# Emptyings ahead of the sum, and more pairs between the steps of a tile, in an attention kernel with four chained stages

## What is computed

```python
h      = x @ W[cat] + b[cat]                       # cond, weights chosen per sequence
q,k,v  = split(h @ w_qkv.T)                        # 16 heads of 32
s      = q k^T / sqrt(32) - |i - j| * slope, masked to -10000 above the diagonal
num    = 0.5 * (1 + s * rsqrt(1 + s*s))            # in the place of exp
attn   = (num / (sum(num) + 1e-6)) @ v ; x1 = x + attn @ w_out.T
z      = layernorm(x1 + relu(x1 @ W1 + b1) @ W2 + b2) * gamma + beta
out    = x1 + int8_matmul(round(z / scale), weight_int8) * scales + bias
```

## Time and profile before

| | |
|---|---|
| median of 3 runs | 2193.9 us (2190.4 to 2200.6) |
| the profiled execution | 2191.51 us, of which the span of instructions is 2189.8 us |
| mean granted TensorE clock | 0.929 of 2.4 GHz |
| busy: PE, DVE, ACT, POOL | 1778.5, 1736.8, 1709.5, 1693.0 us |
| HBM | 31 GB/s over the span |

### The profile page before, as it was taken

How to read it: one execution, slowest core, us unless ns; L and a number is a source line. 1 busy time by engine, 2 the same in 40 slices (tenths; PEclk the granted TensorE clock), 3 DMA queues, 4 the chain that set the end, 5 groups by cost and what they waited for, 6 DMA issues and landing times.

```text
span 2189.8 us, 29394 instructions
## 1 busy us (share of the span) xinstructions
PE 1778.5 (81%) x10699; PEld 901.2 (41%) x10702; DVE 1736.8 (79%) x1730; ACT 1709.5 (78%) x1842; POOL 1693.0 (77%) x723
## 2 busy tenths in 40 slices
PE   5678888888887879997786887888888788988764
PEld 4455434333333445654343443433333344444231
DVE  4248888988999878977555777899999898879748
ACT  0037999999999978977554777999999998889652
POOL 3037899999989968877554776899998998889648
PEclk9899999999999989999988999999999999999889
DMA  5411111111111112212211212011111113112146
GB/s 182 150 50 41 46 31 31 42 38 35 36 35 45 31 56 64 60 41 61 68 44 47 81 50 64 24 44 40 36 32 36 41 31 90 42 57 58 59 160 204
DMA packets 122139, 130.38 MB, mean 60 GB/s; under 512 B 27372, under 2 KB 77548, under 8 KB 121580
## 3 DMA queue, kind: packets, MB, share of 16 engines
q1 hardware_dynamic: 121996, 128.51, 21.0%
HBM read 45.89 MB, written 22.54 MB: 31 GB/s over the span
## 4 chain that ended last, share of the span: by engine, by line
PE 34%; ACT 28%; DVE 17%; issue 11%; POOL 4%; SPq 3%; DMA 2%; DVEq 0%; POOLq 0%; ACTq 0%
ACT yb L765 11%; ACT gb L730 8%; ACT yb L767 8%; DVE gb L1094 6%; PE sc L943 6%; PE ov L921 6%; DVE gb L1159 5%; PE dn L921 5%; PE it L859 4%; PE it L866 4%; PE it L839 3%; SPq L479 3%; POOL oT L724 2%; PE it L843 2%; DMA area<-in_x_dram 1%
## 5 line engine op out<-in xcount | busy, mean ns | idle before, releaser
L691 POOL TENSOR_TENSOR yb<-yb 128x1024 f32<-128x1024 f32 x544 | 1503.6, 2776 | 384.8 <-DVE gb L1159 369.0
L1159 DVE TENSOR_TENSOR gb<-sc,yb 128x1024 f32<-128x1024 f32 x544 | 663.3, 1219 | 170.2 <-ACT yb L767 165.6
L765 ACT ACTIVATE yb<-sc 128x1024 f32<-128x1024 f32 x544 | 550.7, 1012 | 265.0 <-PE sc L943 157.9
L1094 DVE TENSOR_TENSOR gb<-gb,yb 128x1024 f32<-128x1024 f32 x544 | 753.8, 1386 | 0.0
L943 PE MATMUL sc<-qmv,kst 128*128 128x512 f32 (+3 forms) x1280 | 479.7, 458 | 175.0 <-DVE gb L1159 160.7
L767 ACT ACTIVATE yb<-yb 128x1024 f32<-128x1024 f32 x544 | 575.6, 1058 | 17.2
L730 ACT ACTIVATE gb<-gb 128x1024 f32<-128x1024 f32 x544 | 566.2, 1041 | 0.0
L943 PEld LDWEIGHTS sc<-qmv,kst 128*128 128x128 f32 x1280 | 230.6, 202 | 492.9 <-DVE gb L1159 342.8
L921 PE MATMUL ov<-gb,vv 128*32 128x512 f32 (+3 forms) x2560 | 320.0, 584 | 30.2 <-DVE den L1108 22.6
L921 PE MATMUL dn<-gb,ones 128*32 128x512 f32 (+3 forms) x2560 | 310.5, 568 | 0.0
L839 PE MATMUL it<-hT,wT 128*128 128x512 f32 x496 | 249.4, 608 | 14.4 <-ACT area L742 8.5
(11 more groups left out here) (118 smaller groups left out, 1087.9 us busy)
## 6 DMA issues: line engine op xcount, KB each, us to landing
qmv<-stage SPq DMA_DIRECT2D x384, 64.0 KB
kst<-stage SPq DMA_DIRECT2D x384, 64.0 KB
area<-in_x_dram SPq DMA_DIRECT2D x58, 256.0 KB, 2.8
out_dram<-oT SPq DMA_DIRECT2D x32, 256.0 KB, 3.2
wT<-wT_d SPq DMA_DIRECT2D x7, 768.0 KB, 4.3
x_d<-area SPq DMA_DIRECT2D x16, 256.0 KB, 2.6
z_d<-area SPq DMA_DIRECT2D x16, 256.0 KB, 2.9
gb<-z_d SPq DMA_DIRECT2D x4, 1024.0 KB, 12.2
```

The costliest lines, as they stand in the source:

```text
L691: pool.tensor_tensor(y, y, y, ALU.mult).then_inc(s_y2, 1)
L765: act.activation(yview(n), sc[:, n % SLOTS], ACT.Square).then_inc(s_s2, 1)
L1094: dve.tensor_tensor(gview(n), gview(n), yview(n), ALU.add).then_inc(s_num, 1)
L1159: dve.tensor_tensor(gview(n), sc[:, n % SLOTS], yview(n), ALU.mult).then_inc(s_g, 1)
```

## The change

EVAC goes from 1 to 2 and NORMED from 2 to 3: each step of a tile is placed at least two pairs behind the one it needs (zt three pairs behind norm), as far as due pairs allow. On ACT the emptyings of a pair now stand ahead of (1 + g) squared. On DVE the order becomes: product(k-1), outputs, emptyings of pair k, sum(k-3), inversions, product(k). Between the sums and products nothing is moved against each other; what moves are the emptyings and outputs, which now come ahead of the sum. The last three sums instead of two are left for the end.

```diff
-EVAC = 1
-NORMED = 2
+EVAC = 2
+NORMED = 3
...
                     act.activation(yview(n), yview(n), ACT.Abs_reciprocal_sqrt, bias=1.0).then_inc(s_y, 1)
-                    if n >= NUM_LAG:
-                        one_plus_g_squared(n - NUM_LAG)
                     for job in after_pair.get(k, []):
                         d = b if g is ending else b - 1
                         after(d, job, bases[0] + job.index, zs_before(d, job.name[1]))
+                    if n >= NUM_LAG:
+                        one_plus_g_squared(n - NUM_LAG)
...
-                def scored(k):
+                def product(k):
 
                     n = G * PAIRS + k
                     if n >= GRING:
                         dve.wait_ge(s_pv, products_until(n - GRING))
                     dve.wait_ge(s_y, n + 1)
                     dve.tensor_tensor(gview(n), sc[:, n % SLOTS], yview(n), ALU.mult).then_inc(s_g, 1)
+                    for u in emptied.pop(k, []):
+                        c = g.last_unit.index(u % UNITS)
+                        if u >= 0:
+                            output(G, hg, g, u, c, g is opening and c == 0)
+                        else:
+                            output_prev(G, prev_hg, u, c)
+
+                def rest(k):
+
+                    n = G * PAIRS + k - 1
                     if n >= NUM_LAG:
                         numerator(n - NUM_LAG)
                     while reduced and reduced[0][0] < k:
...
+                emptied = {}
                 k = None
                 for e in g.events:
-                    if e[0] in ("qk", "pv") and k is not None:
-                        scored(k)
-                        k = None
                     if e[0] == "qk":
+                        if k is not None:
+                            rest(k)
+                            product(k)
                         k = e[1]
...
                     elif e[0] == "pv":
                         u = e[1]
-                        if u < 0 and not carry:
-                            continue
-                        if u % UNITS in g.last_unit:
-                            c = g.last_unit.index(u % UNITS)
-                            if u >= 0:
-                                output(G, hg, g, u, c, g is opening and c == 0)
-                            else:
-                                output_prev(G, prev_hg, u, c)
-                if k is not None:
-                    scored(k)
+                        if (u >= 0 or carry) and u % UNITS in g.last_unit:
+                            emptied.setdefault(k, []).append(u)
+                rest(k)
+                product(k)
...
-            for n in range(TOTAL - NUM_LAG, TOTAL):
+            for n in range(TOTAL - NUM_LAG - 1, TOTAL):
                 numerator(n)
```

## The result

| | before | after |
|---|---|---|
| median of 4 runs each, same chip | 2192.9 us | 2311.8 us (2311.5 to 2312.8) |
| ratio, 95% interval | | 1.0537 (1.051 to 1.0563) |
| the profiled execution, and its span | 2191.5, 2189.8 us | 2312.8, 2311.0 us |
| mean granted TensorE clock | 0.929 | 0.913 |

What follows compares the result with a forecast made beforehand. ACT was taken to bound plain groups, PE was busiest in closing, joining waited in chains. Plain +15, opening +8, closing +3, joining +10.5, ending +7 gave +43: 2234.5 us, 2237 against the median; range 2184 to 2268.

Steps and rivals of the forecast that it cites:

- part 1: DVE's emptyings ahead of the sum, all groups: sums meet POOL's y squared; plain +15, opening +8, closing +3, joining +8, ending +4.
- part 3: Longer lags in joining and ending: waits for inputs go (-5, -8; -3), forced rows cost (+16, +8, +1.5; +12).
- Of a plain group's 16 emptyings I count 10, since the others fall beside an existing stall.: Plain groups: only 10 emptyings delay the next square, 10 x 0.6 = 6.0 us per group before the outputs' gain.
- 0.6 us late, whether the emptying is short or long: At a moved emptying the sum ends 1.95 us later against 1.34 of slack, so the next square starts 0.6 late.
- covers ACT's delay: Closing group: PE is often the later one; 16 x 0.6 less 6 shorter waits of PE, 1.1 each, gives +3 us.
- The output now precedes a sum of 1.22 us, which gives 1.1 back: Plain groups: PE waits less for outputs, 1.1 us back twice in a group, so 2.2 off each group's 6.0.
- The reading that POOL needs 2.78 us per pair: Profile reading: POOL needs 2.78 us per pair, so has not much to spare of 2.95.
- Rival 3: Much slower: late product holds up PE with PV and item, each emptying costs 1.2 us; 52 more, 2289 us; chance 0.08.
- Part 2: ACT's emptyings ahead of (1+g) squared: banks free 1.04 us earlier; joining -10 us, ending -6.
- joining's pair 67: Forced row of the last tiles' steps at the end of joining: 14.5 + 1.5 for rt.15 = +16 us.
- Pairs 7 and 8: Joining: w2.0, zt.0, w2.1, zt.1 forced in a row at pair 8; 10 less 2 they cost before, +8 us.
- the wait of o for x: Joining: o's emptying waited 19.9 us in four times for x's load; longer lags relieve two of these, -8 us.

## Why the prediction was wrong

The direction and the chain of causes were right, the sum was not: part 1 was sized for single meetings of sum and y squared, too few and too cheap, and part 3 left out the closing group and priced the forced rows too low.

**Part 1 (+38, measured +94).** The mechanism was: a sum behind an emptying meets y squared and ends 1.95 us later against 1.34 of slack. The runs bear that out, and where an emptying stands alone its size too: square to square took 3.57 us in pair 42 (q) and 3.77 in pair 55 (v), 0.6 and 0.8 over 2.95, forecast 0.6. Three terms were mis-sized.
- *"Of a plain group's 16 emptyings I count 10, since the others fall beside an existing stall."* ACT waited for the sum 19 times with the DVE order alone, and 17 times, 13.9 us, in plain group 1 of the changed kernel, for 16 emptyings and 4 outputs. Existing stalls spared three at most, not six.
- *"0.6 us late, whether the emptying is short or long"* was worked out for a pair whose predecessor was on time. In neighbouring pairs it is 1.4 and 1.1 us, as the rows of pairs 28 and 29 show. A pair in which the sum waits y squared out needs 1.9 + 1.1 = 3.0 us for these two alone, where a pair has 2.95, so nothing is made good in it; and POOL stood idle for 2.3 us behind it in pair 55. By group, with the DVE order alone and the forecast in brackets: plain +51 in all (15), opening +19 (8), closing +8 (3), joining +3 (8), ending +11 (4). The plain groups bring 36 of the 56 us. PE "covers ACT's delay" in the closing group only in part: with the DVE order alone ACT waited there for the sum 30 times, 29.4 us, and the group became 8 us longer.
- *"The output now precedes a sum of 1.22 us, which gives 1.1 back."* It gave 1.1 and 1.3 back at two outputs of a plain group and cost 0.6 and 0.8 at the other two, which I had not looked at; the sum behind it took 1.94, for it meets y squared as well. With the outputs alone the four plain groups gained 3 us in all, forecast 8.8, and the whole run lost some 6.

The reading that POOL needs 2.78 us per pair was off too: 0.9 of it is a wait for the sum, as the durations of 1.89 and 2.80 us show.

Rival 3 had the size, "each emptying costs 1.2 us" and 52 us more than forecast, at a chance of 0.08; part 1 came out 56 above. The way there was not the one it named, a late product that holds up PE with PV and item: ACT's waits for the scores of L943 fell, from 157.9 us to 91.3 with the DVE order alone, and what grew are its waits for the sum. That the size came out is luck. I counted stalls and gains as if each stood alone, though I had myself read that DVE and POOL have little to spare. In a plain group POOL, DVE and ACT are busy 90 to 96% of the time, with the waits for each other that these records hold; such a loop does not make a delay good but passes it on.

The Trainium skill's page SBUF — State Buffer (notes to the diagram) says that a DVE operation with two SBUF inputs and a GpSimd operation that reads SBUF exclude each other for a whole instruction. It holds here: with y squared cut, the sum took 1.24 us in the mean at any place, and the cost of the order fell from 94 to 12 us. A rule that the trace bore out was used for the sign and for a single meeting, and not for how the two engines' holds fill the pair.

**Part 2 (-16, measured -17, and -14 in the profiled executions).** Joining fell by 7.8 us (forecast 10), ending with what follows by 6.5 (forecast 6), each from the DVE order alone to both orders. Between the same two runs PE's waits in joining for L742 (at L839) went from 8.5 to 5.6 us in three times each, for L748 from 17.5 to 14.4 in four, and for L745 from 5.1 to 3.1 in four: 0.5 to 1.0 us each, where the forecast had 1.04.

**Part 3 (+21.5, measured +41).** The plan worked out is the one that the kernel has, rows at pairs 8 and 67 included. Of its prices: joining's pair 67 lasted 24.0 us with the lags alone, 21.1 more than before (forecast 16). Two whole chains of a, w2, norm and zt stand in it, 12.7 us in the changed kernel from one zt to the other with rt.15 and a.15 between them, not 10.3 as in the earlier trace rows. The forecast took 3.8 us off the 18.3 of pair 21 for ACT's own work, as only moved; without that it had been 19.8. Pair 62, which was not priced, took 5.6 us more, and the six other pairs from 60 on 7.6 together. Pairs 7 and 8 were priced well: pair 8 took 12.8 us more and pair 7 5.4 less, 7.3 together (forecast 8). PE's waits for the norm (L823 for L682) went from 8.8 us in two times to 27.3 in six. The gains came: the wait of o for x, 19.9 us, is no longer among joining's waits of over 2 us, and by pair 59 the group was 9.3 us ahead in spite of pair 8. Joining alone came to +24.9 (forecast +12.5), ending with what follows to +12 (forecast +9), 11.6 us ahead by pair 60 and 23.6 lost from there on. **The term that was missing is the closing group, +10.6**: EVAC is also the lag of h behind xt, the due pairs there (44 for tile 0 to 59 for tile 15) stand as well, and the forecast went through the plans of joining and ending only. The run with h's lag put back confirms it.

So of the 76 us by which the sum was short, 56 are part 1, 11 the closing group, and the rest the prices of the forced rows. That joining as a whole came near its forecast (+13.5 against +10.5) is luck: the orders gave 5 us, not 2, the lags cost 24.9, not 12.5, and together they cost 6 us less than the two runs add up to.

Of the signs to look for: the mean of the sum 1.57 us (said 1.5) and y squared 2.47; ACT's waits for the sum in a plain group 17, not 10; plain groups 222 to 225 us, not 212 to 214; pair 67 23.6 us in joining, not 15 to 20, and in ending PE waited 5.8 and 4.8 us for the norm there; joining 380, within 350 to 395.

## What to carry to other kernels

Where two engines exclude each other, add up their holds over one period of the loop before moving an instruction between them: here 1.9 + 1.1 of 2.95 us left nothing, so a single meeting cost 0.6 to 0.8 us, and neighbours 1.1 to 1.4 each. An order that pays in a group that waits in chains (joining, 5 us, and 11 with POOL held back) loses where ACT sets the pace (plain groups, 13 us each), so an order is a property of a stage and not of a kernel. And when a constant is changed, list every job that reads it and run the plan of every group: longer lags with fixed due pairs space out the first steps (9.3 us gained in joining by pair 59) and pile up the last ones (34.2 us lost from pair 60 on).

## What was not expected of the hardware

Within a forced row the granted clock falls to the lower of its two levels, 1.2 GHz, and the row's own matmuls become slower. Windows across the row of pair 67, with the columns of the earlier trace rows:

```profile
1447.00:1456.00 9.00, 3.47 (x17) 2.51 (x17) 2.46 (x5) 2.64 (x4) 3.47 (x4) 0.83 0.37 89
1456.00:1464.00 8.00, 4.60 (x13) 2.39 (x11) 1.42 (x3) 2.05 (x6) 1.26 (x1) 0.50 0.12 37
1464.00:1471.00 7.00, 3.73 (x16) 1.94 (x20) 3.92 (x7) 2.61 (x6) 4.36 (x4) 0.50 0.01 2
1471.00:1490.00 19.00, 16.69 (x111) 7.81 (x104) 13.33 (x12) 17.10 (x18) 14.02 (x5) 0.76 0.05 14
```

In the window in which the clock fell PE was busy for 3.5 of 9 us. The clock stayed at 0.50 until the pairs went on, and was at 0.76 in the mean of the next 19 us. The two matmuls of w2 took 1.10 us at 1449.61 and 2.04 at 1460.43, at the lower level. The clock over the joining group was 0.90 before and 0.86 after, and 0.84 with the lags alone, where PE's busy time for the same work rose from 286 to 298 us. The forecast's price, from pair 21, has this in it already: over that row of the kernel before the granted clock was 0.63, over pair 67 here 0.62, and 0.58 with the lags alone. So the clock explains little of what made pair 67 dearer than forecast. How much of the 24 us of pair 67 is clock was not measured by itself.
